# Two graph layers on one core: double uses of adjacency blocks by Strassen's seven products

## The chip, the cores and the metric

The kernel runs on one core of one Trainium2 chip. The metric is the device time of one execution in microseconds, the median over runs.

## What is computed

```python
def reference(x, adj, L0_gnn_u, L1_gnn_weight, L1_gnn_bias):   # x, u (8192, 64), adj (8192, 8192), all float32
    x_drop = x * (u >= 0.1) / 0.9
    h = layernorm(x + adj @ x_drop)                  # first layer
    return layernorm(h + adj @ (h @ weight) + bias)  # second layer
```

adj is 268 MB and every element of it is used twice: once against the dropped x, once against h, and row block i of h exists only when row block i of the first product is complete.

## The kernel before, in words

**Blocks.** adj is cut into 16 x 16 blocks of 512 x 512; one block is a 1 MB tile in SBUF, [128, 4, 512] (4 chunks of 128 of the contraction, 512 output columns). There are `SLOTS` = 17 such tiles. `stat` holds per column block j and chunk c a [128, 128] of which the left 64 columns are x_drop and the right 64 are h. These are the weights; the tile is the moving operand. A matmul has 64 weight columns, so two stand side by side in the array (output partitions 0-63 and 64-127). Every float32 matmul of the program is two records in the profile.

**Jobs.** `order_of_work` (L89) writes out one list of jobs, and every engine walks it. A tile job is one of: `first` (i, j): block against x, 4 matmuls (L591 and L596 alternate, into `sum_a` and `sum_b`). `second`: block against h, 4 matmuls (L637). `pair`: two blocks of one column against h, 8 matmuls (L631). `early`: two blocks against x and h, 16 matmuls (L615). `fused`: one block against x and h at once, a double use, 8 matmuls of 512 columns (L586), into the two halves of `sum_a`. There are 137 first, 71 fused, 59 pair, 24 early, 19 second. `second`, `pair` and `early` write an `echo` bank of PSUM (3 of them), which VectorE adds into `layer1` or `layer2` (`join`, L474); TensorE waits for the bank's last join.

**Order.** In row i the list has the row's double uses j < i (`heavy`), its other blocks (`light`), seconds left over of earlier columns (`again`), and last the blocks near the diagonal (`near`, j = i to i+3; `held`), whose tiles stay in SBUF until h of their column exists. Then `row_end` i: ScalarE and VectorE copy the row's sum to `halves`. Then `FILL` = 6 halves of filler work (a `first` is one half, a pair or a double use two), after the first of which comes `turn` i: 4 transposes (L652), and on VectorE and ScalarE the layernorm (L520 to L528) that gives h of block i. After the filler come the held blocks of column i. A load with `WORK_OF_LOAD` and a job with `WORK_OF_HALF` per half keep a `lead` that the order's rules look at.

**Loads.** `place_tiles` (L156) gives every load a slot; SyncE issues the loads in order of first use (L335), and each waits on SyncE until the job that used the slot before is done (`tile_jobs_done`). There are 334 loads for 256 blocks. At the start x and u are staged in the last four slots (`staged`, L250) in five groups (L313, L314, issued before loads 0, 1, 3, 6 and 10), VectorE drops and scales each (L461, L464), and a load to one of these slots waits until all five are through (`dropped`).

Of the kernel before, what the change touches and what calls it, by code (L numbers as in the profile page):

```python
# [30 lines left out]
P = 128  # L31
N = 8192
D = 64
# [4 lines left out]
EPS = 1e-5  # L38

SLOTS = 17  # L40
EARLY = 4
HOLD = 3
FILL = 6
ECHO_BANKS = 3
WORK_OF_HALF = 11
# [3 lines left out]
AGAIN_KEPT = 4  # L49
LAST_KEPT = 5  # L50
# [20 lines left out]
TILE_JOBS = ("fused", "first", "second", "pair", "early")  # L71
HALVES = {"first": 1, "second": 1, "fused": 2, "pair": 2, "early": 4}
# [12 lines left out]
def has_fused(i):  # L85
    return i >= 2 and i > begins_at(i)


def order_of_work():  # L89
# [6 lines left out]
    def put(job):  # L96
        nonlocal lead
        if job[0] in ("first", "fused", "early"):
# [3 lines left out]
        lead = max(0, min(LEAD_MOST, lead + HALVES[job[0]] * WORK_OF_HALF - n * WORK_OF_LOAD))  # L102
        jobs.append(job)

    for i in range(NB):
# [4 lines left out]
        heavy = [("fused", i, j) for j in range(begins_at(i), i - 1) if i >= 2]  # L110
# [14 lines left out]
        if has_fused(i):  # L125
            heavy.append(("fused", i, i - 1))
        while True:
# [58 lines left out]
def resnorm_graph_layers(nc: bass.Bass, x, adj_t, u, weight, bias, out):  # L186
# [3 lines left out]
    def own_sums(i):  # L190

        return sum(has_fused(r) for r in range(EARLY, i + 1))

# [5 lines left out]
    joined = [job for job in jobs for _ in range({"second": 1, "pair": 1, "early": 2}.get(job[0], 0))]  # L199
# [10 lines left out]
    with ctx:  # L210
# [9 lines left out]
        layer2 = sb("layer2", [P, NB // 2, B])  # L220
        x_res = sb("x_res", [P, 2, C * D])
# [20 lines left out]

        def of_row(i):
            return slice(i % 2 * D, i % 2 * D + D)
# [11 lines left out]
        sum_a = banks[0:2]  # L256
        sum_b = banks[2:4]
        turned = banks[4]
        echo = banks[5:8]

# [23 lines left out]
        layer2_copied = sem("layer2_begun_from_sum_a")  # L284
        layer2_summed = sem("layer2_joined_by_sum_a")
# [12 lines left out]
        y_ready = sem("y_ready")  # L298
        weights_centred = sem("weight_bias_centred")
# [42 lines left out]
        def _(pool):  # L342
# [6 lines left out]
                               base=0, pattern=[[-1, P]], channel_multiplier=1).then_inc(identity, 1)  # L349
            pool.wait_ge(weights_centred, 2)  # L350
# [20 lines left out]
        def _(act):  # L371
# [10 lines left out]
            for job in jobs:  # L382
                if job[0] == "row_end":
# [4 lines left out]
                    if i >= EARLY and i % 2 == 0:  # L388
                        act.activation(halves[D:P, :], sum_b[i % 2][D:P, :], ACT.Copy).then_inc(half_by_act, 1)  # L389
                    else:  # L390
                        act.activation(halves[0:D, :], sum_a[i % 2][0:D, :], ACT.Copy).then_inc(half_by_act, 1)  # L391
                    if has_fused(i) and i < EARLY:

                        act.activation(layer2_block(i), sum_a[i % 2][D:P, :], ACT.Copy).then_inc(layer2_copied, 1)
# [10 lines left out]
        def _(dve):  # L405
# [12 lines left out]
            def centre_weights():  # L418
# [6 lines left out]
                dve.scalar_tensor_tensor(out=bias_b[:, :], in0=row_mean[:, 1:2].to_broadcast([P, D]), scalar=-1.0 / D,  # L425
                                         in1=bias_b[:, :], op0=ALU.mult, op1=ALU.add).then_inc(weights_centred, 1)
# [9 lines left out]
            def variance(squares, var_ap, n):  # L436
                dve.wait_ge(squared, norms)
                step(dve.tensor_reduce(out=vsum[:, 0:n], in_=squares, axis=AX.X, op=ALU.add))  # L438
                dve.tensor_scalar(var_ap, vsum[:, 0:n], 1.0 / D, EPS, ALU.mult, ALU.add).then_inc(var_ready, 1)
# [17 lines left out]
            for n, (begin, end) in enumerate(XU_GROUPS):  # L457
# [6 lines left out]
                dve.tensor_scalar(stat[:, t, 0:D], stat[:, t, 0:D], 1.0 / (1.0 - DROP), None, ALU.mult).then_inc(dropped, 1)  # L464

# [9 lines left out]

            for job in jobs:
                if job[0] == "early":
# [3 lines left out]
                elif job[0] in ("second", "pair"):  # L481
                    last_row = tiles_of(job)[-1][0]
                    if 2 <= last_row < EARLY:
                        dve.wait_ge(layer2_copied, last_row - 1)
                    elif last_row > EARLY:
                        dve.wait_ge(layer2_summed, own_sums(last_row))
# [8 lines left out]
                elif job[0] == "row_end":  # L495
# [4 lines left out]
                    if i < EARLY:  # L500
                        dve.tensor_copy(halves[D:P, :], sum_b[i % 2][D:P, :]).then_inc(half_by_dve, 1)  # L501
                    else:

                        dve.wait_ge(added, n_second)
                        source = sum_b if i % 2 else sum_a
                        dve.tensor_tensor(out=halves[of_row(i), :], in0=source[i % 2][of_row(i), :],  # L506
                                          in1=layer1_pair(i)[of_row(i), :], op=ALU.add).then_inc(half_by_dve, 1)
                        if has_fused(i):
                            dve.tensor_tensor(out=layer2_block(i), in0=sum_a[i % 2][D:P, :], in1=layer2_block(i),
                                              op=ALU.add).then_inc(layer2_summed, 1)  # L510
# [185 lines left out]
```

## Time and profile before

| | us |
|---|---|
| median of 3 runs (lowest, highest) | 946.46 (946.38, 946.99) |
| the profiled execution, its own time | 946.82 |
| its span, first to last instruction | 944.9 |
| TensorE busy | 911.6 |
| VectorE busy | 202.8 |
| ScalarE, GpSimd busy | 29.9, 24.1 |
| transferred | 359.36 MB, mean 380 GB/s |
| TensorE idle on a tile's arrival, all before 73 us | 24.7 |

The span is the time between the first and the last instruction; 1.9 us of the execution lie outside it. Busy time counts matmuls that overlap once. The granted clock is a share of full speed: 1.00 is the level of 2.4 GHz and 0.50 that of 1.2 GHz, and a value between is a stretch that has both.

### The profile page before, as it was taken

Reading aid. Unit: us, or ns where it says so; the run is one execution under the profiler, and the core shown is the slowest. Engines: PE = TensorE matmul, PEld = TensorE weight load, DVE = VectorE, ACT = ScalarE, POOL = GpSimd, SP = SyncE. Lnnn points to the kernel's source line nnn. Section 1 sums busy time; section 2 is a strip of 40 time slices with the busy share of each in tenths; the row PEclk is TensorE's granted clock in tenths of the full one; section 3 lists DMA queues with packets and bytes.
Section 4 is the critical chain, followed back from the end, with each engine's and each line's share of the span. In section 5 each row is a group of like instructions: output and inputs, shape, how many; then the busy total and the mean of one; then the engine's idle time right before and its main releaser. Section 6 shows DMA issues by size and latency. Waiting matters only on the chain.

```text
span 944.9 us, 9819 instructions
## 1 busy us (share of the span) xinstructions
PE 911.6 (96%) x4288; PEld 307.0 (32%) x4288; DVE 202.8 (21%) x419; ACT 29.9 (3%) x68; POOL 24.1 (3%) x23
## 2 busy tenths in 40 slices
PE   4689999999999999999999999999999999999996
PEld 1123333333333333333333333333333333333342
DVE  2111121120131221312213120402122121130256
ACT  0010000000000000000000000000000000000011
POOL 2000000000000000000000000000000000000123
PEclk9799999999999999999999999999999999999998
DMA  9999999999969899799999999998989989999951
GB/s 349 402 421 421 419 421 421 421 385 423 420 273 422 335 377 421 307 421 387 349 412 389 421 363 421 368 421 327 422 343 397 420 347 421 420 418 421 395 225 67
DMA packets 57338, 359.36 MB, mean 380 GB/s; under 512 B 6352, under 2 KB 14544, under 8 KB 14544
## 3 DMA queue, kind: packets, MB, share of 16 engines
q1 hardware_dynamic: 57296, 358.74, 93.3%
q8 instruction: 34, 0.56, 0.2%
q14 instruction: 8, 0.07, 0.0%
HBM read 356.61 MB, written 2.10 MB: 380 GB/s over the span
## 4 chain that ended last, share of the span: by engine, by line
PE 92%; DMA 5%; SPq 3%; DVE 1%; issue 0%; ACT 0%; DVEq 0%
PE psum L586 26%; PE psum L631 22%; PE psum L591 21%; PE psum L615 18%; DMA tiles<-adj_t 5%; PE psum L637 3%; SPq L335 2%; PE psum L652 1%; PE psum L667 1%; SPq L314 1%; PE psum L596 0%; SPq L313 0%; DVE vsum L438 0%; DVE layer L544 0%; DVE rstd L444 0%
## 5 line engine op out<-in xcount | busy, mean ns | idle before, releaser
L591 PE MATMUL psum<-tiles,stat 128*64 128x512 f32 x548 | 252.7, 610 | 24.7 <-DMA tiles<-adj_t 24.7
L586 PE MATMUL psum<-tiles,stat 128*64 128x512 f32 x1136 | 253.3, 593 | 0.0
L596 PE MATMUL psum<-tiles,stat 128*64 128x512 f32 x548 | 252.7, 610 | 0.0
L631 PE MATMUL psum<-tiles,stat 128*64 128x512 f32 x944 | 210.7, 593 | 0.0
L474 DVE TENSOR_TENSOR layer<-psum,layer 128x512 f32<-128x512 f32 (+1 forms) x126 | 87.0, 690 | 461.1 <-PE psum L631 213.5
L615 PE MATMUL psum<-tiles,stat 128*64 128x512 f32 x768 | 169.1, 593 | 0.0
L591 PEld LDWEIGHTS psum<-tiles,stat 128*64 128x64 f32 x548 | 75.4, 140 | 191.0 <-issue 150.1
L586 PEld LDWEIGHTS psum<-tiles,stat 128*64 128x64 f32 x1136 | 80.7, 137 | 158.1 <-issue 158.1
L631 PEld LDWEIGHTS psum<-tiles,stat 128*64 128x64 f32 x944 | 67.2, 137 | 131.7 <-issue 130.9
L615 PEld LDWEIGHTS psum<-tiles,stat 128*64 128x64 f32 x768 | 54.8, 137 | 108.0 <-issue 108.0
L596 PEld LDWEIGHTS psum<-tiles,stat 128*64 128x64 f32 x548 | 75.4, 140 | 0.0
L506 DVE TENSOR_TENSOR halves<-psum,layer 64x512 f32<-64x512 f32 x12 | 8.3, 689 | 146.4 <-PE psum L596 146.4
L637 PE MATMUL psum<-tiles,stat 128*64 128x512 f32 x152 | 35.7, 592 | 0.0
L363 POOL TENSOR_TENSOR x_res<-stat,bias_b 128x512 f32<-128x512 f32 x4 | 5.1, 1273 | 898.1 <-DVE stat L528 884.3
L391 ACT ACTIVATE halves<-psum 64x512 f32<-64x512 f32 x10 | 5.9, 590 | 492.9 <-PE psum L596 492.9
L637 PEld LDWEIGHTS psum<-tiles,stat 128*64 128x64 f32 x152 | 10.9, 137 | 21.7 <-issue 21.7
L520 DVE TENSOR_TENSOR work<-psum,x_res 128x256 f32<-128x256 f32 x16 | 6.8, 423 | 33.9 <-PE psum L652 33.8
L438 DVE TENSOR_REDUCE vsum<-work 128x4 f32<-128x256 f32 (+1 forms) x24 | 12.2, 509 | 8.4 <-ACT work L378 8.4
L494 DVE TENSOR_TENSOR layer<-psum,layer 64x512 f32<-64x512 f32 x19 | 13.2, 694 | 0.7
L461 DVE SCALAR_TENSOR_TENSOR stat<-tiles 128x1024 f32<-128x1024 f32 (+2 forms) x5 | 5.1, 1012 | 33.3 <-DMA tiles<-x 33.3
L389 ACT ACTIVATE halves<-psum 64x512 f32<-64x512 f32 x6 | 3.6, 592 | 271.3 <-PE psum L596 271.3
L501 DVE COPY halves<-psum 64x512 f32<-64x512 f32 x4 | 2.8, 694 | 38.9 <-PE psum L596 38.9
(38 smaller groups left out, 143.3 us busy)
## 6 DMA issues: line engine op xcount, KB each, us to landing
tiles<-adj_t SPq DMA_DIRECT2D x334, 1024.0 KB, 11.4
x_res<-x SPq DMA_DIRECT2D x16, 128.0 KB, 10.6
out<-layer SPq DMA_DIRECT2D x8, 256.0 KB, 2.1
tiles<-u SPq DMA_DIRECT2D x3, 512.0 KB, 14.0
tiles<-x SPq DMA_DIRECT2D x3, 512.0 KB, 15.2
tiles<-u SPq DMA_DIRECT2D x1, 384.0 KB, 6.2
tiles<-x SPq DMA_DIRECT2D x1, 384.0 KB, 7.3
tiles<-u SPq DMA_DIRECT2D x1, 128.0 KB, 2.0
```

What stands on the lines that cost most here:

```text
L314: sp.dma_start(x_stage[:, b], x_v[:, b]).then_inc(s_xu[g], 16)
L335: sp.dma_start(tiles[:, slot], adj_t[i, j]).then_inc(s_arrived[slot], 16)
L438: step(dve.tensor_reduce(out=vsum[:, 0:n], in_=squares, axis=AX.X, op=ALU.add))
L474: return dve.tensor_tensor(out=to, in0=addend, in1=to, op=ALU.add)
L494: dve.tensor_tensor(out=to, in0=bank[D:P, :], in1=to, op=ALU.add).then_inc(added, 1)
L586: last = pe.matmul(sum_a[i % 2][to, :], stat[:, j * C + c, half], tile[:, c], start=begun.get(("a", to.start)) != i, stop=False, skip_grou ...
L591: last = pe.matmul(sum_a[i % 2][low, :], stat[:, j * C + c, 0:D], tile[:, c], start=begun.get(("a", 0)) != i, stop=ends and c == 2, skip_g ...
L596: last = pe.matmul(sum_b[i % 2][high, :], stat[:, j * C + c, 0:D], tile[:, c], start=begun.get(("b", D)) != i, stop=ends and c == 3, skip_ ...
L615: last = pe.matmul(bank[to, :], stat[:, j * C + c, half], tile[:, c], start=c == 0, stop=c == C - 1)
L631: last = pe.matmul(bank[to, :], stat[:, j * C + c, D:2 * D], tile[:, c], start=c == 0, stop=c == C - 1)
L637: last = pe.matmul(bank[to, :], stat[:, j * C + c, D:2 * D], moving[0][:, c], start=c < 2, stop=c >= 2)
L652: last = pe.transpose(turned[:, c * P:(c + 1) * P], halves[:, c * P:(c + 1) * P], ident[:, :])
```

## The change

**The products.** A double use of rows i >= 5 (`fused`, 65 of them; 6 others stay 8 plain matmuls and are called `both`) is the product of a 2 x 2 block matrix: the weights [x|h] of the upper and lower two chunks, against the tile's halves. It is now done with Strassen's seven products in the form with few additions (Winograd's), each product 64 weight columns, 256 moving columns and two chunks: 14 matmuls of 256 columns. They accumulate over the row in two PSUM banks, `products`, and the eight parts of these are combined once per row (`combine`). `first` now puts chunks 0 and 2 in the lower and 1 and 3 in the upper half of one bank, `sum_f`.

**The operand sums.** On VectorE `operands(n)` makes four sums of a tile's quarters ([128, 1024], [128, 512], [128, 512]) in one of two buffers, up to `AHEAD` = 3 jobs before the double use, never before the second last double use is done. `sum_stat(j)` makes the sums of the weights once per column j in 4 to 13, in `stat_homes` or in parts of `layer1` that are free by then. `combine(i)` is 13 operations of [64, 256] after the row's last fused job. h is kept scaled by a constant found from x by reductions behind each staged group.

**The order and the slots.** `SLOTS` 17 becomes 14, so the staged slots are 10 to 13. A double use counts 19 instead of 22 in `lead`, at most two stand in a row where other work is left, and the filler after a row takes seconds left over (`again`) for i > 7, no more double uses.

```diff
-SLOTS = 17
+SCALE_LEAST = 1e-10
+SLOTS = 14
 EARLY = 4
+HOMES = 5
+AHEAD = 3
 HOLD = 3
 FILL = 6
 ECHO_BANKS = 3
-WORK_OF_HALF = 11
+WORK = {"first": 11, "second": 11, "both": 22, "fused": 19, "pair": 22, "early": 44}
 WORK_OF_LOAD = 16
 LEAD = 32
 LEAD_MOST = 40
 AGAIN_KEPT = 4
+MOST_IN_A_ROW = 2
...
-    return i >= 2 and i > begins_at(i)
+    return i > EARLY
+def double(i, j):
+    return ("fused" if has_fused(i) and j < NB - 2 else "both", i, j)
...
-                choice = [heavy, early] if lead < LEAD else []
-                choice = [jobs_of for jobs_of in (*choice, light, again, heavy, early, near) if jobs_of]
+                choice = [early] if lead < LEAD and early else [again] if i > 7 else []
+                choice = [jobs_of for jobs_of in (*choice, light, again, early, heavy, near) if jobs_of]
...
+        summed = not has_fused(i)
+        kept = LAST_KEPT if i == NB - 1 else AGAIN_KEPT
+        in_a_row = 0
         while True:
             due = [job for job in early if job[1] == i]
             if not (heavy or light or due):
                 break
-            if lead < LEAD and (due or heavy or early):
-                chosen = early if due else heavy or early
-            elif len(again) > (LAST_KEPT if i == NB - 1 else AGAIN_KEPT):
+            spare = len(light) + max(0, len(again) - kept) + len(early)
+            if heavy and in_a_row * (spare + 1) < len(heavy) and in_a_row < MOST_IN_A_ROW:
+                chosen = heavy
+            elif lead < LEAD and (due or heavy or early):
+                chosen = early if due else (early or heavy if in_a_row >= MOST_IN_A_ROW else heavy or early)
+                if chosen is heavy and in_a_row >= MOST_IN_A_ROW:
+                    chosen = light or (again if len(again) > kept else heavy)
+            elif len(again) > kept:
                 chosen = again
             elif i == NB - 1:
                 chosen = light or heavy or early
             else:
-                chosen = light or again or (early if due else heavy)
+                chosen = light or (early if due else heavy)
+            in_a_row = in_a_row + 1 if chosen is heavy else 0
             put(chosen.pop(0))
+            if not summed and not any(job[0] == "fused" for job in heavy):
+                jobs.append(("combine", i))
+                summed = True
...
+    sums_from, chain_at = [], 0
+    for job in jobs:
+        if job[0] in ("row_end", "turn"):
+            chain_at = done_after[job]
+        elif job[0] == "fused":
+            n = len(sums_from)
+            begin = max(tile_jobs.index(job) - AHEAD, freed_for[job[1:3], "fused"], chain_at)
+            if n >= 2:
+                begin = max(begin, tile_jobs.index(fused_jobs[n - 2]) + 1)
+            sums_from.append(begin)
...
-        sum_a = banks[0:2]
-        sum_b = banks[2:4]
+        products = banks[0:2]
+        sum_f = banks[2:4]
...
+                dve.wait_ge(dropped, n + 1)
+                for side, op in enumerate((ALU.max, ALU.min)):
+                    dve.tensor_reduce(out=largest[:, side, n:n + 1], in_=stat[:, t, 0:D], axis=AX.XY,
+                                      op=op).then_inc(dve_step, 1)
+                steps += 2
...
+            def sum_stat(j):
+                dve.wait_ge(h_ready, j + 1)
+                t = stat_sums(j)
+                x_j = stat[:, j * C:(j + 1) * C, 0:D]
+                h_j = stat[:, j * C:(j + 1) * C, D:2 * D]
+                step(dve.tensor_tensor(out=t[:, 0:2], in0=h_j.rearrange("p (v k) f -> p v k f", v=2),
+                                       in1=stat[:, j * C:j * C + 2].rearrange("p k (v f) -> p v k f", v=2),
+                                       op=ALU.subtract))
+                step(dve.tensor_tensor(out=t[:, 2], in0=h_j[:, 2:4], in1=t[:, 0], op=ALU.subtract))
+                dve.tensor_tensor(out=t[:, 3], in0=t[:, 2], in1=x_j[:, 2:4],
+                                  op=ALU.subtract).then_inc(stat_sums_ready, 1)
+            def operands(n):
+                _, i, j = fused_jobs[n]
+                if n >= 2:
+                    dve.wait_ge(tile_jobs_done, done_after[fused_jobs[n - 2]])
+                slot, use = place[fused_jobs[n], (i, j)]
+                dve.wait_ge(s_arrived[slot], 16 * (use + 1))
+                tile, a = tiles[:, slot], tile_sums[:, n % 2]
+                step(dve.tensor_tensor(out=a[:, 0:2], in0=tile[:, 0:2].rearrange("p k (v m) -> p v k m", v=2),
+                                       in1=tile[:, :, B // 2:B].rearrange("p (v k) m -> p v k m", v=2), op=ALU.add))
+                step(dve.tensor_tensor(out=a[:, 2], in0=a[:, 1], in1=tile[:, 0:2, 0:B // 2], op=ALU.add))
+                dve.tensor_tensor(out=a[:, 3], in0=tile[:, 2:4, 0:B // 2], in1=a[:, 2],
+                                  op=ALU.add).then_inc(operands_ready, 1)
...
+                dve.tensor_copy(t_0, products[0][low, left]).then_inc(dve_step, 1)
+                plus(first[side, left], products[0][high, left]).then_inc(dve_step, 1)
+                step(plus(second[:, left], products[1][high, right]), 3)
+                step(minus(t_1, products[1][low, left], t_0))
+                plus(first[side, left], t_0).then_inc(dve_step, 1)
+                step(minus(t_2, products[1][high, left], t_1), 2)
+                plus(second[:, left], t_2).then_inc(dve_step, 1)
+                step(minus(t_0, products[0][low, right], t_1, ALU.subtract), 2)
+                step(minus(t_2, products[0][high, right], t_0))
+                minus(first[side, right], products[1][low, right], first[side, right]).then_inc(dve_step, 1)
+                step(plus(second[:, right], products[1][high, left]), 2)
+                plus(first[side, right], t_2).then_inc(combined, 1)
+                plus(second[:, right], t_2).then_inc(combined, 1)
...
+                        new = begun.get("products") != i
+                        begun["products"] = i
+                        if new:
+                            pe.wait_ge(combined, 2 * combined_rows(i - 1))
+                        if j - EARLY + 1 > stat_sums_seen:
+                            pe.wait_ge(stat_sums_ready, j - EARLY + 1)
+                            stat_sums_seen = j - EARLY + 1
+                        n = fused_jobs.index(job)
+                        left, right = slice(0, B // 2), slice(B // 2, B)
+                        a, t = tile_sums[:, n % 2], stat_sums(j)
+                        for k in range(2):
+                            pe.matmul(products[0][low, left], stat[:, j * C + k, 0:D], tile[:, k, left],
+                                      start=new and k == 0, stop=False, skip_group_check=True)
+                            pe.matmul(products[0][high, left], stat[:, j * C + 2 + k, 0:D], tile[:, 2 + k, left],
+                                      start=new and k == 0, stop=False, skip_group_check=True)
+                        pe.wait_ge(operands_ready, n + 1)
+                        pe.matmul(products[0][low, right], t[:, 1, 0], a[:, 0, 0],
+                                  start=False, stop=False, skip_group_check=True)
+                        pe.matmul(products[0][high, right], t[:, 1, 1], a[:, 0, 1],
+                                  start=False, stop=False, skip_group_check=True)
+                        for k in range(2):
+                            pe.matmul(products[1][low, left], t[:, 2, k], a[:, 2, k],
+                                      start=new and k == 0, stop=False, skip_group_check=True)
+                            pe.matmul(products[1][high, left], t[:, 0, k], a[:, 1, k],
+                                      start=new and k == 0, stop=False, skip_group_check=True)
+                        for k in range(2):
+                            pe.matmul(products[1][low, right], t[:, 3, k], tile[:, 2 + k, right],
+                                      start=False, stop=False, skip_group_check=True)
+                            last = pe.matmul(products[1][high, right], stat[:, j * C + 2 + k, D:2 * D], a[:, 3, k],
+                                             start=False, stop=False, skip_group_check=True)
```

Where the change moves instructions, three places. The first is TensorE at one double use, before (L586, where x7 stands for seven more) and now:

```order
L586 MATMUL psum<-tiles,stat 64x512 [waits tile_arrived_9]
L586 MATMUL psum<-tiles,stat 64x512 x7
```

```order
L749 MATMUL psum<-tiles,stat 64x256 [waits products_combined,tile_arrived_0]
L751 MATMUL psum<-tiles,stat 64x256
L749 MATMUL psum<-tiles,stat 64x256
L751 MATMUL psum<-tiles,stat 64x256
L754 MATMUL psum<-tile_sums,stat_homes 64x256 [waits tile_sums_ready]
L756 MATMUL psum<-tile_sums,stat_homes 64x256
L759 MATMUL psum<-tile_sums,stat_homes 64x256
L761 MATMUL psum<-tile_sums,stat_homes 64x256
L759 MATMUL psum<-tile_sums,stat_homes 64x256
L761 MATMUL psum<-tile_sums,stat_homes 64x256
L764 MATMUL psum<-tiles,stat_homes 64x256
L766 MATMUL psum<-tile_sums,stat 64x256
```

(L764 and L766 come once more.) 8 matmuls of 512 columns are 14 of 256, and from the fifth on they wait for VectorE's sums.

The second is SyncE at the start: the last staged group (L313, L314 before, L370, L371 now) and the loads behind it. Before, then now:

```order
L313 DMA tiles<-u 128x4x256
L314 DMA tiles<-x 128x4x256
L335 DMA tiles<-adj_t 128x2048 x3
L335 DMA tiles<-adj_t 128x2048 [waits x_dropped] x3
```

```order
L370 DMA tiles<-u 128x4x256
L371 DMA tiles<-x 128x4x256
L392 DMA tiles<-adj_t 128x2048 [waits x_dropped] x4
```

The three loads that stood ahead of the wait for VectorE's drop are behind it.

The third is TensorE around the end of row 10: the last `near` job, the filler with the transposes, and the first held block. Before:

```order
L591 MATMUL psum<-tiles,stat 64x512 [waits tile_arrived_13]
L596 MATMUL psum<-tiles,stat 64x512
L591 MATMUL psum<-tiles,stat 64x512
L596 MATMUL psum<-tiles,stat 64x512
L586 MATMUL psum<-tiles,stat 64x512 [waits half_of_row_summed,layer2_joined_by_sum_a,half_of_row_copied,tile_arrived_7]
L586 MATMUL psum<-tiles,stat 64x512 x7
L652 MATMUL psum<-ident,halves 128x128 [waits half_of_row_summed,half_of_row_copied,turned_read]
L652 MATMUL psum<-ident,halves 128x128 x3
L586 MATMUL psum<-tiles,stat 64x512 [waits tile_arrived_9]
L586 MATMUL psum<-tiles,stat 64x512 x7
L586 MATMUL psum<-tiles,stat 64x512 [waits tile_arrived_1]
L586 MATMUL psum<-tiles,stat 64x512 x7
```

And now:

```order
L731 MATMUL psum<-tiles,stat 64x512 [waits tile_arrived_12]
L731 MATMUL psum<-tiles,stat 64x512 x3
L800 MATMUL psum<-tiles,stat 64x512 [waits second_added,tile_arrived_9,tile_arrived_7]
L800 MATMUL psum<-tiles,stat 64x512 x7
L824 MATMUL psum<-ident,halves 128x128 [waits half_of_row_summed,half_of_row_copied,turned_read]
L824 MATMUL psum<-ident,halves 128x128 x3
L800 MATMUL psum<-tiles,stat 64x512 [waits second_added,tile_arrived_4,tile_arrived_0]
L800 MATMUL psum<-tiles,stat 64x512 x7
L800 MATMUL psum<-tiles,stat 64x512 [waits second_added,tile_arrived_9,tile_arrived_7]
L800 MATMUL psum<-tiles,stat 64x512 x7
L806 MATMUL psum<-tiles,stat 64x512 [waits second_added,h_ready,tile_arrived_1]
L806 MATMUL psum<-tiles,stat 64x512 x3
```

The filler was three double uses with one new tile each; it is three pairs with two new tiles each, and the third pair's tiles go into slots 9 and 7, which the first pair has just used.

## Rows read from the trace of the kernel before

**Rows 1.** The page: busy time of TensorE; times it ran, share of the span.
```profile
span 944.9 us, 9819 instructions
PE 911.6 (96%) x4288; PEld 307.0 (32%) x4288; DVE 202.8 (21%) x419; ACT 29.9 (3%) x68; POOL 24.1 (3%) x23
```

**Rows 2.** Stretches: length, TensorE busy (records), granted clock, DMA share, GB/s.
```profile
75.00:100.00 25.00, 25.00 (x120) 1.00 1.01 421
200.00:300.00 100.00, 100.00 (x470) 1.00 0.92 378
700.00:900.00 200.00, 200.00 (x936) 1.00 0.98 398
```

**Rows 3.** The chain of waits, 857 to 890 us: start, length, records.
```profile
857.43 24.03 PE psum L586 x112
883.18 3.43 PE psum L631 x16
886.61 0.59 PE psum L652 x4
```

**Rows 4.** Groups of instructions: busy us, mean ns of one, idle before.
```profile
L586 PEld LDWEIGHTS psum<-tiles,stat 128*64 128x64 f32 x1136 | 80.7, 137 | 158.1 <-issue 158.1
L667 PE MATMUL psum<-w,layer 64*128 64x128 f32 x128 | 9.1, 284 | 0.0
L667 PEld LDWEIGHTS psum<-w,layer 64*128 64x128 f32 x128 | 7.7, 187 | 5.7 <-issue 5.7
```

**Rows 5.** Timeline of TensorE, the last matmuls: start, length.
```profile
934.22 2.12 PE L667 MATMUL psum<-w,layer 64*128 64x128 f32 x32
```

**Rows 6.** Timelines of SyncE and VectorE at the last staged group: start, length.
```profile
24.34 1.79 SPq L314 DMA_DIRECT2D tiles<-x  x1
26.18 8.55 SPq L335 DMA_DIRECT2D tiles<-adj_t  x1
...
41.94 1.23 DVE L461 SCALAR_TENSOR_TENSOR stat<-tiles 128x1024 f32<-128x1024 f32 x1 [11.11 <-DMA tiles<-x]
43.20 0.69 DVE L464 TENSOR_SCALAR stat<-stat 128x1024 f32<-128x1024 f32 x1
...
43.92 1.28 SPq L335 DMA_DIRECT2D tiles<-adj_t  x3
```

**Rows 7.** Timeline of TensorE, four waits for a tile: length, idle before in brackets.
```profile
20.91 0.64 PE L591 MATMUL psum<-tiles,stat 128*64 128x512 f32 x1 [2.45 <-DMA tiles<-adj_t]
31.39 1.12 PE L591 MATMUL psum<-tiles,stat 128*64 128x512 f32 x1 [3.42 <-DMA tiles<-adj_t]
44.44 1.11 PE L591 MATMUL psum<-tiles,stat 128*64 128x512 f32 x1 [3.08 <-DMA tiles<-adj_t]
72.66 0.64 PE L591 MATMUL psum<-tiles,stat 128*64 128x512 f32 x1 [0.56 <-DMA tiles<-adj_t]
```

**Rows 8.** The tiles at 300 to 330 us: issue of a load to landing.
```profile
DMA to landing us min/median/max: 4.7/10.5/12.6
```

**Rows 9.** Stretches around those waits, columns as in rows 2.
```profile
31.00:37.00 6.00, 5.61 (x14) 0.50 1.00 417
44.40:48.00 3.60, 3.56 (x10) 0.57 1.02 426
48.00:72.60 24.60, 19.39 (x84) 1.00 1.01 420
```

**Rows 10.** Groups of instructions on VectorE, by shape.
```profile
L544 DVE TENSOR_TENSOR layer<-layer,rstd 128x512 f32<-128x512 f32 x1 | 0.7, 691 | 0.0
L474 DVE TENSOR_TENSOR layer<-psum,layer 128x512 f32<-128x512 f32 x107 | 74.0, 691 | 412.7 <-PE psum L631 213.5 <-PE psum L615 196.2 <-issue 2.1
L432 DVE SCALAR_TENSOR_TENSOR work<-sums,work 128x256 f32<-128x256 f32 x16 | 6.8, 425 | 0.5
```

**Rows 11.** Timeline of VectorE, steps that wait for the one before.
```profile
501.53 0.42 DVE L522 TENSOR_TENSOR work<-psum,work 128x256 f32<-128x256 f32 x1
501.99 0.42 DVE L431 TENSOR_REDUCE sums<-work 128x4 f32<-128x256 f32 x1
```

More of the change, by code:

```diff
@@ L68, in seconds_of @@
     return jobs
-TILE_JOBS = ("fused", "first", "second", "pair", "early")
-HALVES = {"first": 1, "second": 1, "fused": 2, "pair": 2, "early": 4}
+TILE_JOBS = ("fused", "both", "first", "second", "pair", "early")
+HALVES = {"first": 1, "second": 1, "both": 2, "fused": 2, "pair": 2, "early": 4}
 def tiles_of(job):
@@ L97, in put @@
         nonlocal lead
-        if job[0] in ("first", "fused", "early"):
+        if job[0] in ("first", "both", "fused", "early"):
             n = len(tiles_of(job))
@@ L109, in order_of_work @@
             light.insert(0, ("first", 1, 0))
-        heavy = [("fused", i, j) for j in range(begins_at(i), i - 1) if i >= 2]
+        heavy = [double(i, j) for j in range(begins_at(i), i - 1) if i >= 2]
         if i >= 1:
@@ L188, in resnorm_graph_layers, with combined_rows @@
     loads, place = place_tiles(jobs)
-    def own_sums(i):
-        return sum(has_fused(r) for r in range(EARLY, i + 1))
+    def combined_rows(i):
+        return sum(has_fused(r) for r in range(i + 1))
     done_after, n_tile_jobs = {}, 0
@@ L198, in resnorm_graph_layers @@
         done_after[job] = n_tile_jobs
-    joined = [job for job in jobs for _ in range({"second": 1, "pair": 1, "early": 2}.get(job[0], 0))]
+    fused_jobs = [job for job in jobs if job[0] == "fused"]
+    tile_jobs = [job for job in jobs if job[0] in TILE_JOBS]
+    latest_freed, freed_for = 0, {}
+    for load in loads:
+        latest_freed = max(latest_freed, load[4])
+        freed_for[load[0:2], load[5]] = latest_freed
+    sums_from, chain_at = [], 0
[8 more added lines that the diff above has]
+            sums_from.append(begin)
+    joined = [job for job in jobs for _ in range({"second": 1, "both": 1, "pair": 1, "early": 2}.get(job[0], 0))]
     finals = [job[1] for job in jobs if job[0] == "final"]
@@ new lines, in combine, with plus, minus @@
+            def combine(i):
+                low, high = slice(0, D), slice(D, P)
+                left, right = slice(0, B // 2), slice(B // 2, B)
+                side = of_row(i)
+                t_0, t_1 = [work[side, n].rearrange("p c d -> p (c d)") for n in range(2)]
+                t_2 = third[side, :]
+                first, second = layer1_pair(i), layer2_block(i)
+                def plus(to, addend):
+                    return dve.tensor_tensor(out=to, in0=addend, in1=to, op=ALU.add)
+                def minus(out, product, addend, op1=ALU.add):
+                    return dve.scalar_tensor_tensor(out=out, in0=product, scalar=-1.0, in1=addend, op0=ALU.mult, op1=op1)
+                dve.tensor_copy(t_0, products[0][low, left]).then_inc(dve_step, 1)
[11 more added lines that the diff above has]
+                plus(second[:, right], t_2).then_inc(combined, 1)
@@ new lines, in _ @@
+            for job in jobs:
+                if job[0] in TILE_JOBS:
+                    while n_operands < len(fused_jobs) and sums_from[n_operands] <= n_tile_jobs:
+                        operands(n_operands)
+                        n_operands += 1
+                    n_tile_jobs += 1
+                if job[0] == "combine":
+                    i = job[1]
+                    dve.wait_ge(tile_jobs_done, done_after[job])
+                    dve.wait_ge(added, n_second)
+                    combine(i)
+                    n_combined += 1
+                    dve.wait_ge(combined, 2 * n_combined)
+                elif job[0] == "early":
@@ L480, in _ @@
                     join(layer2[:, job[1] // 2], echo[n_second % ECHO_BANKS]).then_inc(added, 1)
-                elif job[0] in ("second", "pair"):
+                elif job[0] in ("second", "both", "pair"):
                     last_row = tiles_of(job)[-1][0]
[L483 to L486, printed above, removed]
                     dve.wait_ge(tile_jobs_done, done_after[job])
@@ L602, in _ @@
+                    if kind != "both":
+                        last.then_inc(tile_jobs_done, 1)
+                if kind == "early":
                     _, i, j = job
@@ L617, in _ @@
                     last.then_inc(tile_jobs_done, 1)
-                elif kind in ("second", "pair"):
+                elif kind in ("second", "both", "pair"):
                     _, i, j = job
@@ L640, in _ @@
                     n_second += 1
-                elif kind == "row_end":
-                    first_of_row = True
+                elif kind == "row_end" and job[1] == 0:
+                    pe.wait_ge(identity, 2)
+                    pe.wait_ge(x_reduced, 1)
+                    pe.matmul(scale_sum, mean_of_partitions, largest[:, 0, len(XU_GROUPS):],
+                              start=True, stop=True).then_inc(scale_summed, 1)
                 elif kind == "turn":
```

132 lines of the change are left out of this document (75 added, 57 removed).

## The prediction, written before the changed kernel was run

> **What bounds the kernel now.** I read the page's busy times first: TensorE works 911.6 us of a span of 944.9 [rows 1]. Then a table of stretches, to see whether that is one regime: from 75 us to past 900 TensorE is busy in the whole of every stretch at the full clock, while the DMA engines move 378 to 398 GB/s where the start shows 421 at their limit [rows 2]. So TensorE bounds the middle, with 5 to 10% of DMA rate to spare. Up to 72.6 us it is the other way: TensorE waits for tile after tile [rows 7] and the DMA engines run at 420 [rows 9]. A microsecond taken from TensorE's work after 73 us comes off the end unless a tile, a sum or a bank is late; a microsecond of DMA time lost before 73 us is added to the end.
>
> The chain of waits gives TensorE's pace: 112 records of 512 columns in 24.03 us, 0.2146 each, a double use of 16 records 3.43 us [rows 3]. At 2.4 GHz 512 columns are 0.2133, so 0.0013 per record is fixed. One tile of 1.049 MB at 421 GB/s takes 2.49 us.
>
> **The saving.** 65 double uses become 28 records of 256 columns. At 0.1067 + 0.0013 = 0.108 each a double use takes 3.02 us: 0.41 less, 26.7 us in all. No row has 256 columns, so I bound it. Above: twice the pace of 512 exactly, 3.00 us, saves 27.9. Below: the nearest short matmuls are the last 32 records, 128 columns each, 2.12 us from first start to last end, of which 0.27 is one record's own length [rows 4, 5]: 1.85 over 30 further records is 0.062, 0.008 over the 0.0533 of 128 columns. At 0.1067 + 0.008 a use takes 3.22 and 13.9 us are saved. There the weight loads set the pace, 7.7 us over 128 records, 0.060 each; the 64-column loads of a double use take 80.7 over 1136, 0.071 [rows 4], well under 0.1067. They stay hidden, so I take 26.7.
>
> The Trainium skill (TensorE: Matmul & The Clock Gate, "Back-to-back issue gap") says that in a stream of weight loads and matmuls both set the spacing, about 81 ns at N = 128 where the matmul alone has about 56. As an estimate from that page, 25 ns more on each of 28 records, two side by side, would be 0.35 us per use and eat 23 of the 27 us. The trace's short matmuls do show such a surplus, a smaller one.
>
> **The first wait (fill).** Before, three loads stand between the last staged group and the wait for VectorE's drop; now none, as the second place of the order shows. The group's drop starts at 41.94 and ends at 43.89, and SyncE issues the waiting load at 43.92 [rows 6]; meanwhile the three loads kept the queues full, and the first landed for the matmul at 44.44 [rows 7]. Now that load is itself issued at 43.92. An issue into empty queues lands after 4.7 us at the least [rows 8], so at 48.6: 4.2 us later. The other bound: if the group lands 2.49 earlier for having no tile beside it, 1.7. The DMA engines idle for it and the fill is theirs, so +4.2. The reductions behind each group's drop (two per group) run in VectorE's gaps of 8 us and more between groups, at no cost.
>
> **The second wait (slots).** 334 loads stay 334. At the end of a row 4+3+2+1 = 10 tiles are held for column uses. 17 slots left 7 for work in flight, 14 leave 4. Before, the filler was double uses, one tile for 3.43 us, more than 2.49. Now it is pairs, two tiles (4.98) for 3.43. At the third place of the order the third pair needs the slots of the first pair: both loads are issued when that pair ends and land 4.7 + 2.49 = 7.2 us later [rows 8], while TensorE has the transposes, 0.59, and the second pair, 3.43 [rows 3]. It waits 3.2. That pattern stands behind row blocks 10, 11 and 12: 9.5 us. Going through the list job by job with 0.43 us per pair of records, 2.49 per load and 2.2 from a freed slot to the first byte (4.7 less 2.49) I find ten smaller waits of 0.5 to 1.1, in rows 6 to 13, 6 us together. The same sum over the list before has none after 75 us, as its trace has none. Bounds: 8 (the small ones vanish) to 20 (half a microsecond more per freed slot, 2% on a load). I take 15.5.
>
> **The clock.** The idle times of 3.08 and 3.42 us before a tile were followed by the 1.2 GHz level, the one of 2.45 was not [rows 7]: granted 0.57 over 3.6 us and 0.50 over 6 us [rows 9], costs of 1.5 and 3.0 us. My three waits of 3.2 lie there, a little less by the profile's count, since the modelled end of a matmul lies 0.16 after its pace. Between 0 and 9 us; I take 2.5. The long gap in the fill brings the same level, but the fill is bound by DMA.
>
> **VectorE.** Per double use, passes of 1024, 512 and 512 elements: 1.23 [rows 6], 0.69 and 0.69 [rows 10], and 0.04 between steps that wait for each other [rows 11], 2.73 us, 177 us in all. `combine` is 13 operations of 0.42 with 8 such steps, 5.8 us for 11 rows; `sum_stat` about 1 us for 10 columns. Busy goes from 203 to some 450 us, half the span. At nothing on the path: the buffers allow a pass to start when the second last use is done, and 3.02 of the last and 0.86 of the first four matmuls cover it; a join of 0.69 may come between [rows 10]. In the 22 places where three uses stand in a row 2.73 must fit into 3.02 each; it does, by 0.3. `combine` hides behind the `near` jobs of the row, 6.9 us; in row 14 behind two of them and a pair, 6.9 against 5.8 + 0.7 for the row's sum. If that cover goes, the transposes are late by the difference. The scale of h adds under 1 us, none of it where TensorE waits.
>
> **Sum.** -26.7 + 4.2 + 15.5 + 2.5 = -4.5 on the profiled execution's 946.8 (span 944.9 and 1.9 around it): 942.3. The median of the runs is 0.4 lower: **942 us**. A measurement can tell about 0.2%, 1.9 us.
>
> **The rivals.**
> (a) *Loads bind, slower.* Every load that waits for a slot takes 1 us longer than the fastest one seen, and 2% is lost on the rate. The slot waits grow by 11.5 us: 953. For it: 4.7 is a minimum, and the median from issue to landing is 10.5 with a queue ahead [rows 8]. Against: after a wait for a slot the queues are near empty. It decides from about 0.8 us more per wait. Chance 0.15.
> (b) *Weight loads pace short matmuls, slower.* 3.22 us per use instead of 3.02: +13, 955. For: the surplus of rows 5. Against: loads of 0.071 under 0.1067 [rows 4]. The skill's rule above is this rival's. 0.10.
> (c) *Sums late, slower.* If a pass takes 3.4 us, for reads of a tile beside TensorE and DMA, the 22 places lose 0.4 each, 9: 951. 0.07.
> (d) *Waits mostly absent, faster.* Fill 1.7, slot waits 8, no clock drop: -26.7 + 9.7 = -17, 929. For: with 5 to 10% of DMA rate spare [rows 2] the list may run ahead of my count. 0.13.
> Forecast 0.55: 934 (slot waits at 8) to 950 (slot waits at 20, clock 6), of it 0.42 faster, 0.09 within 0.2%, 0.04 slower.
>
> **How the numbers follow.** Faster: 0.42 + 0.13 = 0.55. Within: 0.09 + 0.03 from (a) and (c) = 0.12. Slower: 0.33. The range takes the forecast, most of (a) to (c) and (d): 929 to 957.
>
> **What would show it.** Matmuls L749 to L766: 0.108 per record, a double use 3.0 us, TensorE busy near 885 us. One gap of about 7 us near 41 us with a DMA slice under 0.5. Waits for adj tiles at L800 of 3 us behind rows 10 to 12 (about 600, 650 and 705 us), and after them a clock of 0.5 in a stretch of 3 us. Waits for L584 or L604 to L619 near nothing. I am wrong if double uses take over 3.1 us, if TensorE waits for VectorE by more than 3 us in all, or if tile waits after 80 us are under 8 or over 20 us.

## The result, and the profile after

The changed kernel took 955.8 us in the median of four runs (950.9 to 959.4) against 946.6 before: ratio 1.009, 95% interval 1.0069 to 1.0112. It is slower by 0.9%, where 942 was forecast. The profiled execution is the slowest of the four, 959.4 us, span 957.6.

The page of the changed kernel, for [rows 1], with the granted clock and the transfer rate in 40 slices of the span:

```profile
span 957.6 us, 11872 instructions
PE 895.0 (93%) x5070; PEld 378.1 (39%) x5070; DVE 448.4 (47%) x804; ACT 28.7 (3%) x66; POOL 24.2 (3%) x24
...
PEclk9989999999999999999998999999899999999998
...
GB/s 350 302 423 421 421 417 410 388 310 377 421 286 377 421 277 422 421 419 386 326 422 318 420 371 421 331 400 329 362 365 332 422 364 419 422 419 421 421 411 76
```

TensorE is busy 16.6 us less than before, yet the span is 12.7 us longer. (I had expected it busy near 885; it is 895.0, mainly because the lower clock stretches its matmuls.) The timeline of TensorE gives the pace of a double use (start, length), two in a row; each begins with an L749:

```profile
804.48 0.38 PE L749 MATMUL psum<-tiles,stat 128*64 128x256 f32 x1
...
804.70 0.38 PE L749 MATMUL psum<-tiles,stat 128*64 128x256 f32 x1
...
807.50 0.38 PE L749 MATMUL psum<-tiles,stat 128*64 128x256 f32 x1
```

From 804.48 to 807.50 is 3.02 us, as forecast, and a pair of records follows every 0.22 us. So 26.7 us were saved, and the loss is elsewhere. The same timeline has these waits (idle before, in brackets): the fill, and the large ones behind rows 8, 10, 11 and 12.

```profile
49.11 5.27 PE L731 MATMUL psum<-tiles,stat 128*64 128x512 f32 x12 [7.58 <-DMA tiles<-adj_t]
...
512.51 4.54 PE L800 MATMUL psum<-tiles,stat 128*64 128x512 f32 x10 [3.08 <-issue]
...
616.81 1.50 PE L800 MATMUL psum<-tiles,stat 128*64 128x512 f32 x4 [3.32 <-issue]
...
669.65 2.83 PE L800 MATMUL psum<-tiles,stat 128*64 128x512 f32 x6 [3.28 <-issue]
...
726.62 5.30 PE L800 MATMUL psum<-tiles,stat 128*64 128x512 f32 x16 [3.28 <-issue]
```

The profile puts the last four down to "issue", but the chain of waits shows what they are, here behind row 8 (start, length):

```profile
494.76 15.18 DMA tiles<-adj_t
509.94 2.57 issue
512.51 3.65 PE psum L800 x7
```

One tile of the pair lands at 509.94, and the matmuls start 2.57 us later. That is the time of one more load, so I read the rest of the wait as the pair's other tile. And the stretches around them (TensorE busy, granted clock, DMA share, GB/s, for [rows 2, 9]):

```profile
37.00:50.00 13.00, 4.76 (x18) 0.77 0.60 219
510.00:520.00 10.00, 7.49 (x22) 0.66 0.56 231
610.00:620.00 10.00, 6.68 (x26) 0.87 0.91 351
620.00:630.00 10.00, 10.00 (x53) 0.96 0.86 343
660.00:670.00 10.00, 6.72 (x34) 0.93 0.68 259
670.00:680.00 10.00, 10.00 (x36) 0.73 0.69 271
720.00:730.00 10.00, 6.72 (x24) 0.83 0.93 347
```

Each of these four waits is followed by the 1.2 GHz level. Counting a stretch's length times the missing share of the clock, 3.4 us are lost behind row 8 (10 us at 0.66), 1.7, 3.4 and 1.7 behind the next three, 10.2 in all. Over 80 to 900 us TensorE was idle 21.0 us by such stretches of 10 us (before: 0.0), and 2.5 us more hide in the busy count, since the modelled end of the matmul ahead of each of 16 waits lies 0.16 us late (16 records of 3.43 us by their pace show as 3.60). The first `pair` after the fill began at 80.1 us, before at 74.4.

| term, us | forecast | measured on the profiled execution |
|---|---|---|
| 65 double uses | -26.7 | -26.7 |
| fill | +4.2 | +5.7 |
| waits for tiles, 80 to 900 us | +15.5 | +23.5 |
| clock after those waits | +2.5 | +10.2 |
| sum | -4.5 | +12.7 |

The table is of the slowest of the four executions. In the others the granted clock is higher, 0.983 (957.5 us), 0.986 (954.0) and 0.988 (950.9) against 0.981, so part of the 10.2 is missing from the median of 955.8.

### The profile page after: what moved, and what is told of

The parts are those of the page before. It is cut to its first block, busy times and chain, and to the rows that moved or that the text cites. A ratio compares the mean times of both kernels' runs of the same rounds, so it can differ in the third digit from the quotient of the medians.

```text
span 957.6 us, 11872 instructions
## 1 busy us (share of the span) xinstructions
PE 895.0 (93%) x5070; PEld 378.1 (39%) x5070; DVE 448.4 (47%) x804; ACT 28.7 (3%) x66; POOL 24.2 (3%) x24
## 4 chain that ended last, share of the span: by engine, by line
PE 83%; DMA 12%; SPq 3%; issue 2%; DVE 1%; ACT 0%; DVEq 0%
PE psum L800 20%; PE psum L731 20%; PE psum L784 17%; DMA tiles<-adj_t 10%; PE psum L749 5%; PE psum L764 5%; PE psum L759 5%; PE psum L806 4%; PE psum L754 3%; SPq L392 2%; DMA tiles<-x 2%; PE psum L839 1%; PE psum L824 1%; PE psum L751 0%; PE psum L761 0%
## 5 line engine op out<-in xcount | busy, mean ns | idle before, releaser
L731 PE MATMUL psum<-tiles,stat 128*64 128x512 f32 x1144 | 263.5, 603 | 38.1 <-DMA tiles<-adj_t 38.1
L800 PE MATMUL psum<-tiles,stat 128*64 128x512 f32 x944 | 220.8, 615 | 13.8 <-issue 13.8
L784 PE MATMUL psum<-tiles,stat 128*64 128x512 f32 x768 | 169.2, 593 | 0.6 <-issue 0.6
L731 PEld LDWEIGHTS psum<-tiles,stat 128*64 128x64 f32 x1144 | 81.4, 138 | 202.0 <-issue 137.3
L800 PEld LDWEIGHTS psum<-tiles,stat 128*64 128x64 f32 x944 | 71.4, 141 | 145.1 <-issue 143.7
L581 DVE TENSOR_TENSOR tile_sums<-tiles 128x1024 f32<-128x1024 f32 x65 | 79.5, 1223 | 66.9 <-DMA tiles<-adj_t 37.6
L784 PEld LDWEIGHTS psum<-tiles,stat 128*64 128x64 f32 x768 | 55.5, 137 | 108.1 <-issue 108.1
L751 PE MATMUL psum<-tiles,stat 128*64 128x256 f32 x260 | 66.7, 379 | 0.0
L749 PE MATMUL psum<-tiles,stat 128*64 128x256 f32 x260 | 66.7, 379 | 0.0
L766 PE MATMUL psum<-tile_sums,stat 128*64 128x256 f32 x260 | 66.7, 379 | 0.0
L806 PE MATMUL psum<-tiles,stat 128*64 128x512 f32 x200 | 47.3, 594 | 1.5 <-DMA tiles<-adj_t 1.5
L759 PE MATMUL psum<-tile_sums,stat_homes 128*64 128x256 f32 x180 | 46.2, 379 | 0.0
L761 PE MATMUL psum<-tile_sums,stat_homes 128*64 128x256 f32 x180 | 46.2, 379 | 0.0
L764 PE MATMUL psum<-tiles,stat_homes 128*64 128x256 f32 x180 | 46.2, 379 | 0.0
L584 DVE TENSOR_TENSOR tile_sums<-tiles,tile_sums 128x512 f32<-128x512 f32 x65 | 45.0, 692 | 2.2
L583 DVE TENSOR_TENSOR tile_sums<-tile_sums,tiles 128x512 f32<-128x512 f32 x65 | 45.0, 692 | 2.2
L749 PEld LDWEIGHTS psum<-tiles,stat 128*64 128x64 f32 x260 | 35.6, 137 | 26.2 <-issue 13.3
L751 PEld LDWEIGHTS psum<-tiles,stat 128*64 128x64 f32 x260 | 35.6, 137 | 0.0
L766 PEld LDWEIGHTS psum<-tile_sums,stat 128*64 128x64 f32 x260 | 35.6, 137 | 0.0
L759 PEld LDWEIGHTS psum<-tile_sums,stat_homes 128*64 128x64 f32 x180 | 24.7, 137 | 11.4
```

What stands on the lines that cost most here:

```text
L581: step(dve.tensor_tensor(out=a[:, 0:2], in0=tile[:, 0:2].rearrange("p k (v m) -> p v k m", v=2), in1=tile[:, :, B // 2:B].rearrange("p (v ...
L731: last = pe.matmul(sum_f[i % 2][to, :], stat[:, j * C + c, 0:D], tile[:, c], start=begun.get("f") != i and c < 2, stop=ends and c >= 2, sk ...
L749: pe.matmul(products[0][low, left], stat[:, j * C + k, 0:D], tile[:, k, left], start=new and k == 0, stop=False, skip_group_check=True)
L751: pe.matmul(products[0][high, left], stat[:, j * C + 2 + k, 0:D], tile[:, 2 + k, left], start=new and k == 0, stop=False, skip_group_check ...
L759: pe.matmul(products[1][low, left], t[:, 2, k], a[:, 2, k], start=new and k == 0, stop=False, skip_group_check=True)
L761: pe.matmul(products[1][high, left], t[:, 0, k], a[:, 1, k], start=new and k == 0, stop=False, skip_group_check=True)
```

## Experiments

Ratios are to the kernel before, run on the same chip (946.6 to 947.1 us), with 95% intervals. Two theories: **F**, the new filler, three pairs with two loads each, meets four free slots; **S**, 14 slots starve any order.

**1. The kernel before with 14 slots.**

```diff
-SLOTS = 17
+SLOTS = 14
```

> The kernel before with 14 slots for 17 and nothing else; its order of work stays. Theory F (the filler): the waits for tiles after 80 us come from fillers of three pairs, two loads each, that meet four free slots; this order fills with double uses, one load each, so it has no tile wait after 85 us and pays only for the fill, where the loads behind the last staged group now wait for the drop: 946.6 + 4.7 to 5.7 = 951 to 952. Theory S (the slots alone): 14 slots starve any order, 15 to 20 us of tile waits after 85 us and 960 us or more.

956.2 us, 1.0099 (1.0082 to 1.0115). The waits are F's rather than S's: after 80 us they are 3.8 us in all, none above 0.91. The time is 4 us above F's 951 to 952. Its timeline has the gap of the fill and the two longest waits of rows 8 and 9, which F had at none:

```profile
48.46 1.12 PE L591 MATMUL psum<-tiles,stat 128*64 128x512 f32 x1 [7.62 <-DMA tiles<-adj_t]
...
504.98 3.65 PE L586 MATMUL psum<-tiles,stat 128*64 128x512 f32 x16 [0.89 <-DMA tiles<-adj_t]
...
552.37 3.65 PE L586 MATMUL psum<-tiles,stat 128*64 128x512 f32 x16 [0.91 <-DMA tiles<-adj_t]
```

Up to 80 us it is idle 30.2 us, the kernel before 24.7; with the 3.8 later and what the busy count hides of each wait that is the 10.3 us by which the span grew. Of S this much is true: three slots less cost 9 to 10 us by themselves, some 5 of it in the fill (the first job on h after it starts at 79.3 us, before at 74.4).

**2. Double uses done plainly.** Order, slots and loads of the changed kernel, but 8 matmuls of 512 columns for each of the 65.

```diff
 def has_fused(i):
-    return i > EARLY
+    return False
...
-        lead = max(0, min(LEAD_MOST, lead + WORK[job[0]] - n * WORK_OF_LOAD))
+        as_fused = job[0] == "both" and job[1] > EARLY and job[2] < NB - 2
+        work = WORK["fused" if as_fused else job[0]]
+        lead = max(0, min(LEAD_MOST, lead + work - n * WORK_OF_LOAD))
```

> The changed kernel, same order and 14 slots, with its 65 double uses done as 8 plain matmuls of 512 columns (no sums of tile quarters, no combining). Theory F: the products save 65 x 0.41 = 26.7 us whether or not there are waits, so this is 26 to 28 us slower than the changed kernel, near 982, with the same waits of 3 us before the same pairs. Rival: the saved time was mostly given back in waits for loads; then this is only 10 to 15 us slower and its waits are under 10 us in all.

980.8 us, 1.0358 (1.0341 to 1.0376): 25.0 us above the changed kernel. That is a little under the 26 to 28 expected. It waits 20.3 us from 80 to 900, nearly as long as with the products (21.0), and lost 5.1 us there to the clock instead of 10.2. The waits behind rows 10 to 12 are the same (3.29, 3.24 and 3.50 us), the one behind row 8 is not: it is 0.79 us here and 3.08 with the products, and smaller waits have grown in its place. In sum the products' saving is real and was not eaten by waits; order and slots cost 34 us by themselves.

**3. The last staged group earlier.**

```diff
-XU_BEFORE = (1, 3, 6, 10)
+XU_BEFORE = (1, 3, 5, 7)
```

> The changed kernel with the staged groups issued before loads 1, 3, 5 and 7 instead of 1, 3, 6 and 10. Theory F: three loads stand between the last group and the wait for the drop again, the gap of 7.6 us at 41 us goes to about 3 us, and the end comes 5 to 6 us earlier, near 950. Rival (the lead lost in the fill is no loss, since loads bind later): within 2 us of the changed kernel.

950.0 us in the median of 10 runs (946.6 to 953.7), 1.003 (1.0017 to 1.0044), 5.7 less than the changed kernel. Idle time up to 80 us fell from 33.0 to 24.8, as before the change, and the first `pair` starts at 74.4 again; the gap of 7.6 us is one of 2.4. The waits after stayed (21.2). The clock took 3.4 us after 80 us in its profiled execution, so its 948.3 against 959.4 is not the fill alone.

**4 and 5. TensorE kept busy in the waits.** Six matmuls of 512 columns, overwritten afterwards, ahead of a pair that waits.

```diff
+KEEP_WARM = {("pair", 2, 7): 3, ("pair", 4, 9): 3, ("pair", 4, 10): 3, ("pair", 4, 11): 3}
...
+                    if job in KEEP_WARM:
+                        pe.wait_ge(added, n_second - ECHO_BANKS + 1)
+                        bank = echo[n_second % ECHO_BANKS]
+                        for _ in range(KEEP_WARM[job]):
+                            for to in slice(0, D), slice(D, P):
+                                pe.matmul(bank[to, :], stat[:, 0, 0:D], stat[:, 0:C, :], start=True, stop=True)
```

> The changed kernel with 6 matmuls of 512 columns whose product is overwritten (2.6 us of work) ahead of the four pairs that waited 3.1 to 3.3 us for their tiles, so that TensorE is not idle there. The output stays the same. Theory C: those waits cost the clock, 10.2 us in the profiled run, and the draw of how long it stays down makes the runs scatter from 951 to 959. Then this runs at 946 to 949, the runs agree within 1.5 us, and the granted clock is 1.00 from 80 to 900 us. Rival: the clock falls for another reason; then 955 and the same scatter.

952.5 us (949.7 to 955.3), 1.0059 (1.0036 to 1.0081), above the 946 to 949 expected, and the runs spread by 5.6 us. The first of the four sets stood at the wrong pair. In this timeline, behind row 8, the wait is ahead of the matmuls' place, and behind row 10 it is filled:

```profile
511.39 5.35 PE L807 MATMUL psum<-tiles,stat 128*64 128x512 f32 x16 [2.93 <-issue]
...
517.25 1.08 PE L795 MATMUL psum<-stat 128*64 128x512 f32 x4
...
611.60 2.75 PE L795 MATMUL psum<-stat 128*64 128x512 f32 x12
614.91 3.65 PE L807 MATMUL psum<-tiles,stat 128*64 128x512 f32 x16 [0.57 <-issue]
```

16 records at full clock span 3.65 us; behind the unfilled wait they span 5.35. The stretches say the same:

```profile
510.00:515.00 5.00, 3.61 (x10) 0.66 0.78 319
...
612.00:617.00 5.00, 4.43 (x22) 1.00 1.02 424
617.00:622.00 5.00, 5.00 (x26) 1.00 0.92 357
```

The clock stayed up at the three filled waits. Besides row 8 it fell once more, behind row 13, after an unfilled wait of only 2.03 us (1.7 us lost), in the timeline and in the stretches:

```profile
780.32 10.07 PE L807 MATMUL psum<-tiles,stat 128*64 128x512 f32 x38 [2.03 <-issue]
...
778.00:783.00 5.00, 2.97 (x12) 0.82 0.94 357
783.00:790.00 7.00, 7.00 (x32) 0.88 0.97 366
```

Then with the first set moved to `("pair", 0, 7)`:

> As the run with the overwritten matmuls, but the set that stood ahead of the second filler pair behind row 8 now stands ahead of the first, where the wait of 3 us really is. In that run the clock still fell at that place and not where the waits were filled. Theory C: now it falls at none of the four places, clock loss from 80 to 900 us 0 to 1 us (3.4 there, 10.2 in the changed kernel), 948 to 951, and what scatter is left comes from the 7.6 us wait in the fill. Rival: the clock falls elsewhere instead and the time stays at 952 to 953.

951.3 us (950.7 to 953.2), 1.0052 (1.0035 to 1.0068). Clock loss from 80 to 900 us is 0.0, and the spread of the runs went from 8.5 us to 2.5, with four runs of each kernel. The waits themselves are not cured: 13.0 us idle are left and 10.3 are dummy work, 2.3 more than the 21.0 before. What went is the clock's part. The median is 4.5 us lower, the profiled execution 7.9: 10.2 of clock less those 2.3.

**6. The filler of before, its double uses plain.**

```diff
-                choice = [early] if lead < LEAD and early else [again] if i > 7 else []
-                choice = [jobs_of for jobs_of in (*choice, light, again, early, heavy, near) if jobs_of]
-                filler.append(choice[0].pop(0))
+                choice = [heavy, early] if lead < LEAD else []
+                choice = [jobs_of for jobs_of in (*choice, light, again, heavy, early, near) if jobs_of]
+                job = choice[0].pop(0)
+                filler.append(("both",) + job[1:] if job[0] == "fused" else job)
```

> The changed kernel, 14 slots, with the filler rule of the kernel before: three double uses, one load each, fill the turn of a row. Those 27 (of 65) are done as 8 plain matmuls, since their sums could not be ready behind the layernorm; 38 keep Strassen's products. Theory F: without pairs that need two tiles from four free slots the waits after 85 us fall from 21 to under 5 us and the clock stays up (10 us in the profiled run, about 7 in the median), at a price of 27 x 0.41 = 11 us: 955.8 - 17 - 7 + 11 = about 942. Rival (the slots alone starve the order): waits stay above 12 us and the time is 955 or more.

943.7 us in the median of 10 runs (942.6 to 946.5), 0.9972 (0.9962 to 0.9981). Idle from 80 to 900 us is 7.6 instead of 21.0, a little more than the 5 expected, clock loss there 0.0. The 11 us more work on TensorE do not explain that by themselves: experiment 2 has 27 us more and waits 20.3. With 40% of the double uses given up and the same 14 slots it is 12 us faster than the changed kernel. F holds.

**7 and 8. A fifteenth slot.**

```diff
-SLOTS = 14
+SLOTS = 15
-HOMES = 5
+HOMES = 4
+NO_HOME = 12
...
-                step(dve.tensor_tensor(out=a[:, 2], in0=a[:, 1], in1=tile[:, 0:2, 0:B // 2], op=ALU.add))
-                dve.tensor_tensor(out=a[:, 3], in0=tile[:, 2:4, 0:B // 2], in1=a[:, 2],
+                third_sum = tile[:, 0:2, B // 2:B]
+                step(dve.tensor_tensor(out=third_sum, in0=a[:, 1], in1=tile[:, 0:2, 0:B // 2], op=ALU.add))
+                dve.tensor_tensor(out=a[:, 2], in0=tile[:, 2:4, 0:B // 2], in1=third_sum,
...
-                t_2 = third[side, :]
+                t_2 = halves[side, 0:B // 2]
```

> The changed kernel with 15 slots. The room comes from writing one of the four sums over a quarter of the tile that no matmul reads any more, the third partial of the combination in the halves buffer, and one home of weight sums less (column 12: its 3 double uses are plain, 1.2 us). Theory F: five free slots hold half of the third pair's tiles before it is due, so its wait falls from 3.2 to about 0.5 us; waits after 85 us go from 21 to under 6, with them the fallen clock, and the fill gains 1 or 2 us: 955.8 - 16 - 7 + 1 - 1 = 931 to 935. Rival (the loads as a whole bind after the saving, at 93% of their rate): a slot more shifts the waits only, 948 or more.

932.6 us (930.8 to 932.9), 0.9843 (0.9829 to 0.9858), as F expected. Idle from 80 to 900 us is 6.9, clock loss there 0.0. The longest wait, 2.43 us, is behind row 10; behind rows 11 and 12 0.71 and 0.80 are left. With the staged groups of experiment 3 as well:

> Both: 15 slots and the staged groups before loads 1, 3, 5 and 7. Theory F: a further 4 to 5 us less than with 15 slots alone, 926 to 930, below both kernels, runs within 1 us of each other, since no wait of 3 us is left to lower the clock. Rival: the early group only helps where the fill had no slot to spare; same as 15 slots alone.

929.5 us (928.3 to 932.7), 0.9821 (0.9799 to 0.9844): the version that beats both. The gain over the fifteenth slot alone is 3.1 us, less than the 4 to 5 expected, and the intervals overlap. Its page, and the two waits of over 1 us that it has after 80 us:

```profile
span 927.6 us, 11795 instructions
PE 885.5 (95%) x5034; PEld 373.6 (40%) x5034; DVE 443.9 (48%) x798; ACT 28.7 (3%) x66; POOL 24.2 (3%) x24
```

```profile
500.90 3.65 PE L801 MATMUL psum<-tiles,stat 128*64 128x512 f32 x16 [2.85 <-issue]
...
597.77 2.79 PE L801 MATMUL psum<-tiles,stat 128*64 128x512 f32 x12 [1.90 <-issue]
```

Idle from 80 to 900 us is 7.0, clock loss there 0.0, though one wait is of 2.85 us. "No wait of 3 us is left" was nearly right; the runs still spread by 4.4 us, where I had said 1.

## Why the prediction was wrong

**The saving** was right to the hundredth: 3.02 us per double use. Rival (b), weight loads pacing short matmuls, is out; a load of 64 columns is 137 ns as before [rows 4] and stays under the pace. The estimate from the Trainium skill's spacing at N = 128 (TensorE: Matmul & The Clock Gate, "Back-to-back issue gap") is not borne out at 256 columns: it would have given 3.37 us per use, and 3.02 were measured.

**VectorE** was right: 448 us busy against "some 450", passes of 1.22, 0.69 and 0.69 us, and none of TensorE's waits ends on a sum. Rival (c) is out.

**The fill** was named and undersized, 4.2 for 5.7. The last group's drop began at 42.28, not 41.94 [rows 6], the load behind it was issued at 44.26, and its tile reached TensorE at 49.11, 4.85 after the issue (I had 4.7). That makes 4.7 at this tile (44.44 before, [rows 7]). The last microsecond is not the lower clock behind the gap of 7.6 us, for the loads lost it. Stretches of the changed kernel, then of the kernel before (TensorE busy, granted clock, DMA share, GB/s):

```profile
40.00:46.00 6.00, 1.53 (x8) 0.82 0.11 27
46.00:49.00 3.00, 0.00 (x0) 0.50 0.97 399
49.00:80.00 31.00, 25.89 (x102) 0.92 1.01 422
```

```profile
40.00:46.00 6.00, 2.92 (x12) 0.84 1.03 417
46.00:49.00 3.00, 3.00 (x14) 0.75 1.02 426
49.00:80.00 31.00, 25.72 (x114) 1.00 1.01 421
```

From 40 to 49 us 2.4 MB less were moved, which at 421 GB/s is 5.7 us, the whole cost; from 49 us on both run at the same rate. The fill was the loads', as I had said, but I priced how late one tile came instead of how long the transfers stood still.

**The slots**: "I take 15.5" is the first failed step; 23.5 were measured, above my bound of 20. The 8.0 us lie in three places. Behind rows 10 to 12 my 3.2 was 3.5 (609.84 plus 3.43 us for the second pair, then 616.81), 0.9 in all. The wait behind row 8 was one of my small ones, 0.5, and measured 3.1, or 3.2 with the hidden 0.16: 2.7. The largest part, 4.4, is the other small waits: I had nine more with 5.5 us, and there are twelve with 9.9 (8.0 idle and 0.16 hidden in each). Behind row 8 the loads had run at 420 to 426 GB/s without a break from 480 to 510 us and were late by the rate; experiment 2, where TensorE has more work per load, has only 0.79 there. My count had them some 2.7 us further ahead. That it summed small errors on the way is likely but not shown.

**The clock**: "I take 2.5" is the second failed step; 10.2 were measured. My rows had idle times of 3.08 and 3.42 followed by the lower level, and my waits lay beside the first of them [rows 7, 9]; the nearest row said that each costs 1.5 to 3.0, so 4.5 to 9 us for three. I halved it for no reason that a row gave. A fourth wait, the one behind row 8, then lowered it too. Experiment 5 shows the clock's part by itself, 10.2 us in the profiled run and at least 4.5 in the median. It also made most of the spread of 8.5 us: from 0.988 at 950.9 us to 0.981 at 959.4 the granted clock alone is 6.7.

Rival (b)'s 955 came nearest to 955.8 by number, which is luck, since its mechanism did not occur. Rival (a), 953, has the right place, the waits for loads, but for a reason that only half fits: its microsecond per freed slot did not show (0.3 did), and it had no clock in it. Rival (d), waits mostly absent, is out: it had 8 us of them.

What stays open is what decides, at a wait of 2 to 3.5 us, whether the clock falls and for how long: it took 1.7 us at one wait of 3.28 and 3.4 at another.

## What to carry to other kernels

When arithmetic is bought with memory, price the buffers first: here the products saved 26.7 us, and the three slots they took, with an order whose filler needed six tiles where four slots were free, cost 34 (experiment 2). A wait of 3 us on TensorE can cost 5 to 7, when the engine comes back at half clock. That happened at 9 of the 13 unfilled waits of 2.8 to 3.6 us that the runs have from 80 to 900 us, 1.6 us each on average over all 13, and at none of the seven of experiments 4 and 5 that were filled, wholly or in part. So look for work to put into such a wait, or shorten it. And a buffer that seems one too large can sometimes be found again: a quarter of the tile that nobody reads any more gave half a slot.

## What the runs showed that was not expected

The length of a wait does not settle whether the clock falls. In experiment 3 the waits behind rows 8, 10, 11 and 12 were 2.94, 3.52, 3.43 and 2.94 us; the stretches that hold them are

```profile
505.00:515.00 10.00, 8.74 (x34) 0.83 0.60 243
610.00:620.00 10.00, 9.73 (x40) 0.84 0.82 316
663.00:673.00 10.00, 9.96 (x48) 1.00 0.95 342
715.00:725.00 10.00, 7.80 (x38) 1.00 0.98 372
```

and it fell at the first two only. Experiment 8 has one of 2.85 us without a fall, experiment 4 one of 2.03 us with a fall. Clock loss in single executions of the changed kernel differs by 7 us (granted clock 0.981 at 959.4 us, 0.988 at 950.9). Only the first of these has a trace, so that its waits were the same in the other is not shown. A kernel with a few such waits needs more runs than one without.
